# One transfer per weight tile from SyncE instead of two halves from SyncE and GpSimd, and the residual reloads moved to GpSimd's queue

## What is computed

```python
x = layernorm(x + attn(x))        # 16 heads, grouped (8 groups) qkv and output projections
x = layernorm(x + ffn(x))

def attn(x):   # q is scaled by 64 ** -0.5
    a = softmax(q @ k.T) @ v
    return grouped_linear(a, w_proj, b_proj)

def weight_quant(w):
    scale = 1.0 / clip(mean(abs(w)), 1e-05)
    return clip(round(w * scale), -1, 1) / scale

def act_quant(x):
    scale = 127.0 / clip(max(abs(x), -1), 1e-05)
    return clip(round(x * scale), -128, 127) / scale

def ffn(x):    # w_gate, w_up: 4096 x 1024, w_down: 1024 x 4096
    h = silu(act_quant(x) @ weight_quant(w_gate).T) * (act_quant(x) @ weight_quant(w_up).T)
    return act_quant(h) @ weight_quant(w_down).T
```

## Time and profile before

| | us |
|---|---|
| median of 2 runs | 2184.82 (2184.07 to 2185.58) |
| the profiled execution's own time | 2179.08 |
| its span on the slowest core (core 4) | 2177.4 |
| spans of the 8 cores | 2153.1 to 2177.4 |
| TensorE busy | 1348.4 (62%) |
| ScalarE busy | 948.9 (44%) |
| VectorE busy | 924.4 (42%) |
| GpSimd busy | 98.3 (5%) |

### The profile page before, as it was taken

One profiled execution on the slowest core, in us unless ns is written; L12 is line 12 of the kernel. 1 busy time (PEld: TensorE's weight loads), 2 busy tenths in 40 slices (PEclk: granted clock), 3 DMA queues, 4 the chain that ended last, 5 costly groups with the idle time before them and its releaser, 6 DMA issues.

```text
span 2177.4 us, 20832 instructions; the slowest of 8 cores (2153.1 to 2177.4 us)
## 1 busy us (share of the span) xinstructions
PE 1348.4 (62%) x5439; PEld 465.0 (21%) x5502; DVE 924.4 (42%) x1742; ACT 948.9 (44%) x1079; POOL 98.3 (5%) x180
## 2 busy tenths in 40 slices
PE   0057677567747670037673599964999737676682
PEld 0011111111111110011111244421444313222231
DVE  1148830635475323366345644444444441203023
ACT  1167788488838881018882022255112361001011
POOL 0000000001101111111110000000000000000000
PEclk9999888688858785558876799986999968888996
DMA  6789940136634666663651533334244416676672
GB/s 178 225 253 328 314 151 1 39 97 181 184 109 130 175 174 175 163 174 107 170 170 39 140 78 78 76 99 135 56 95 96 120 80 169 158 197 178 173 221 82
DMA packets 379140, 314.04 MB, mean 144 GB/s; under 512 B 298129, under 2 KB 300177, under 8 KB 376978
## 3 DMA queue, kind: packets, MB, share of 16 engines
q1 hardware_dynamic: 339712, 209.80, 37.2%
q0 software_dynamic: 16128, 54.54, 7.7%
q10 hardware_dynamic: 23186, 48.38, 6.5%
HBM read 161.49 MB, written 83.89 MB: 113 GB/s over the span
## 4 chain that ended last, share of the span: by engine, by line
PE 39%; DMA 18%; DVE 14%; ACT 13%; issue 7%; SPq 6%; ACTq 2%; DVEq 1%; POOL 0%; POOLq 0%
PE ps L84 39%; ACT A L84 12%; DVE A L84 10%; SPq L84 6%; DMA A<-wd 4%; DMA A<-wg 3%; DMA wdqT_s<-wtstage 2%; DVE ln_sb L84 2%; DMA wtstage<-wdq_s 2%; ACTq L84 2%; DMA wdt_sb<-wdqT_s 2%; DMA A<-wqkv 2%; DMA A<-wproj 1%; DMA xre_f<-xp_s 1%; DVE h L84 1%
## 5 line engine op out<-in xcount | busy, mean ns | idle before, releaser
L84 ACT ACTIVATE A<-ps,cst_sb 128x1024 bf16<-128x1024 f32 (+1 forms) x544 | 553.4, 1104 | 300.2 <-DVE A L84 209.8
L84 PE MATMUL ps<-A,A 64*128 64x512 bf16 (+1 forms) x2048 | 532.2, 434 | 205.6 <-ACT A L84 180.2
L84 PE MATMUL ps<-wg_sl,xqT 128*128 128x512 bf16 x1003 | 264.4, 408 | 114.6 <-DVE h L84 98.9
L84 PE MATMUL ps<-wdt_sb,hqT 128*128 128x512 bf16 x1003 | 243.6, 400 | 110.4 <-DMA wdt_sb<-wdqT_s 50.0
L84 PEld LDWEIGHTS ps<-A,A 64*128 64x128 bf16 (+1 forms) x2048 | 125.8, 106 | 610.1 <-issue 606.9
L84 ACT ACTIVATE A<-ps,scg 128x512 f32<-128x512 f32 x128 | 87.9, 687 | 331.5 <-PE ps L84 309.5
L84 DVE TENSOR_SCALAR A<-A,wsc 128x1024 f32<-128x1024 f32 x96 | 72.4, 754 | 280.1 <-DMA A<-wg 134.5
L84 DVE SCALAR_TENSOR_TENSOR h<-ps,scu,A 128x512 bf16<-128x512 f32 x128 | 96.1, 751 | 215.9 <-ACT A L84 211.7
L84 PE MATMUL ps<-wproj_sb,A 64*128 64x128 bf16 x256 | 36.4, 274 | 207.7 <-DVE A L84 207.7
L84 PEld LDWEIGHTS ps<-wg_sl,xqT 128*128 128x128 bf16 x1024 | 104.1, 103 | 251.8 <-issue 145.8
L84 DVE TENSOR_SCALAR A<-A 128x1024 f32<-128x1024 f32 (+1 forms) x208 | 144.4, 694 | 30.6 <-DVE A L84 20.0
(11 more groups left out here) (69 smaller groups left out, 756.0 us busy)
## 6 DMA issues: line engine op xcount, KB each, us to landing
wdt_sb<-wdqT_s SPq DMA_DIRECT2D x128, 256.0 KB, 3.5
A<-wg SPq DMA_DIRECT2D x32, 512.0 KB, 7.7
A<-wu SPq DMA_DIRECT2D x32, 512.0 KB, 7.0
A<-wd SPq DMA_DIRECT2D x32, 512.0 KB, 8.7
hq_s<-h ACTq DMA_DIRECT2D x16, 1024.0 KB, 3.9
A<-x SPq DMA_DIRECT2D x16, 512.0 KB, 7.2
xt_s<-A POOLq DMA_DIRECT2D x16, 512.0 KB, 3.8
A<-xt_s ACTq DMA_DIRECT2D x16, 512.0 KB, 3.6
```

The lines of the kernel that those rows point to most:

```text
L84: ins = getattr(eng, meth)(*args, **kw)
```

## The change

Three things, and nothing else for the kernel as it is run (`debug` is off):

1. The load of a weight-quantization unit is one DMA of 128x1024 floats (512 KB) from SyncE. GpSimd no longer issues a half or waits for `c_wq3`, and VectorE waits for one semaphore.
2. The loads of `xre_f` in `emit_down` and their waits go from ScalarE's list to GpSimd's.
3. The bias load has a semaphore of its own (`s_bp`), and waits for the constants ask for 16 instead of 32.

```diff
-    n = dma("scalar", A12[0:1, 0:1024], bproj_d[:, :], "s_cst")
+    n = dma("scalar", A12[0:1, 0:1024], bproj_d[:, :], "s_bp")
...
-    wait("tensor", "s_cst", 32)
+    wait("tensor", "s_bp", 16)
...
         if gidx >= 2:
             wait("sync", "c_wq3", 3 * (gidx - 1), future=True)
-            wait("gpsimd", "c_wq3", 3 * (gidx - 1), future=True)
         else:
             wait("sync", "c_wma", 96, future=True)
-            wait("gpsimd", "c_wma", 96, future=True)
-        dma("sync", stg[:, 0:512], tii[:, 0:512], f"s_wqp{par}")
-        dma("gpsimd", stg[:, 512:1024], tii[:, 512:1024], f"s_wqg{par}")
+        dma("sync", stg, tii, f"s_wqp{par}")
...
             wait("vector", f"s_wqp{par}", 16 * (gidx // 2 + 1))
-            wait("vector", f"s_wqg{par}", 16 * (gidx // 2 + 1))
...
-            wait("scalar", "s_xps0", 16 * (T // 2))
-            wait("scalar", "s_xps1", 16 * (T // 2))
+            wait("gpsimd", "s_xps0", 16 * (T // 2))
+            wait("gpsimd", "s_xps1", 16 * (T // 2))
             if gbase >= 1:
-                wait("scalar", "c_r2", gbase * 4, future=True)
-                wait("scalar", "c_s", c("c_s"))
-                wait("scalar", "s_out0", 16 * 2 * gbase)
-                wait("scalar", "s_out1", 16 * 2 * gbase)
+                wait("gpsimd", "c_r2", gbase * 4, future=True)
+                wait("gpsimd", "c_s", c("c_s"), future=True)
+                wait("gpsimd", "s_out0", 16 * 2 * gbase)
+                wait("gpsimd", "s_out1", 16 * 2 * gbase)
             for t4 in range(2):
-                E.dma("scalar", xre_f[:, t4 * 1024:(t4 + 1) * 1024],
+                E.dma("gpsimd", xre_f[:, t4 * 1024:(t4 + 1) * 1024],
                       xp_s[row0 + t4 * 128: row0 + (t4 + 1) * 128, :], "s_xre")
...
-                    wait("scalar", "c_r2", gbase * 4 + 2, future=True)
+                    wait("gpsimd", "c_r2", gbase * 4 + 2, future=True)
```

More of the change, by code:

```diff
@@ L501, in build @@
             wait("scalar", "m_qkv", c("m_qkv"))
-            wait("scalar", "s_cst", 32)
+            wait("scalar", "s_cst", 16)
             dap = dest[:, p * 2048 + qt * 512: p * 2048 + qt * 512 + 512]
@@ L708, in build @@
             if debug and qc >= 1:
-                wait("scalar", "s_dbg", c("s_dbg"))
+                wait("scalar", "s_dbgA", c("s_dbgA"))
             arp = A8[:, p * 512:(p + 1) * 512]
@@ L741, in build @@
         if debug:
-            wait("vector", "s_dbg", c("s_dbg"))
+            wait("vector", "s_dbgA", c("s_dbgA"))
         em("vector", "reciprocal", A10[:, 64:128], A10[:, 0:64], inc=("c_rcp", 1))
@@ L746, in build @@
             wait("sync", "c_pve", c("c_pve"))
-            dma("sync", dbg_ar[:, :], A8[:, :], "s_dbg")
+            dma("sync", dbg_ar[:, :], A8[:, :], "s_dbgA")
         if attn_lvl < 3 and attn_lvl not in (6, 7):
@@ L797, in build @@
                 wait("sync", "c_radd", c("c_radd"))
-                dma("sync", dbg_rc[:, :], A10[:, :], "s_dbg")
+                dma("sync", dbg_rc[:, :], A10[:, :], "s_dbgA")
             if attn_lvl != 4:
@@ L843, in build @@
         wait("sync", "s_dbg", c("s_dbg"))
-        wait("sync", "s_dbg", c("s_dbg"))
+        wait("sync", "s_dbgA", c("s_dbgA"))
     def wu_slice_ap(par, ic):
@@ L1050, in emit_down @@
                 if t4 == 2:
-                    wait("scalar", "c_r2", gbase * 4 + 2, future=True)
+                    wait("gpsimd", "c_r2", gbase * 4 + 2, future=True)
                     for t4b in range(2, 4):
-                        E.dma("scalar", xre_f[:, (t4b - 2) * 1024:(t4b - 1) * 1024],
+                        E.dma("gpsimd", xre_f[:, (t4b - 2) * 1024:(t4b - 1) * 1024],
                               xp_s[row0 + t4b * 128: row0 + (t4b + 1) * 128, :],
```

## The result

| | before | after |
|---|---|---|
| median, us | 2189.15 (8 runs) | 2127.13 (9 runs) |
| ratio, 95% interval | | 0.9714, 0.9681 to 0.9746 |
| span of the slowest core in the profiled execution | 2177.4 | 2120.8 |
| mean of the eight spans | 2164.6 | 2114.3 |

The change is 2.9% faster, some 62 us by the medians, where 26.5 us and 1.2% were forecast; 2127 lies under the range's lower end of 2130. The direction and the place were right, the size was not. Some executions are a few per cent longer, at a lower granted clock; the ratios and their intervals leave them out, the medians of this table don't, and e7's profile is of such an execution, so that only its cores 0 to 3, whose clock was not lower, are read.

A forecast was written before the change was run, and what follows sets the result against it. VectorE's weight units, waiting for transfers, were taken to hold up TensorE in blocks 1 and 2. Terms: 8.4 - 4.8 + 7.2 + 19.5 - 4.8 + 1.0 = 26.5 us, for a median of 2158 us, range 2130 to 2192.

The forecast's parts named there:

- The place and the edges: Weight units on VectorE hold up about 119 us of block 2 and 7.3 of block 1; block 3 isn't held up.
- Part 1, the unit load: Block 2, seven loads not behind transposes: one load landing in 4.8 us gains 1.2 us each, 8.4 us.
- Part 1, the load behind the transposes: Block 2, six loads behind the fourth transpose in SyncE's queue: twice the bytes, 0.8 us more each, -4.8 us.
- Part 2, the batches: Block 2, five later transpose batches: freed from the late store they fall from 17.4 to 13.5 us, 19.5 us gained.
- Block 1: Pairs of units sharing two buffers win 1.2 us each, 17 us, of which only 7.2 us can be had.
- Part 3: Down products, xre_f reloads moved to GpSimd: each of four groups waits 1.2 us longer, -4.8 us.
- +1.0: Start of the down products: the very first reload pair leaves its place where TensorE waits for down weights, 1 us gained.
- the wide load wins everywhere: Rival: loads behind transposes also land in 4.8 us (+14), batches give +23; 49 us gained, 2136 us; chance 0.18.

The follow-up runs named there:

- e7: Wide unit load alone, issued by GpSimd instead of SyncE, xre_f reloads left on ScalarE, against the kernel before: ratio 0.9966.
- e10: The kernel before with all 32 w_down transposes moved from block 2 to block 3: ratio 0.9714, block 2 at 243.8 us.
- e11: The changed kernel with all w_down transposes moved from block 2 to block 3: ratio to before 0.9531, block 2 at 222.0 us.
- e3: The kernel before with both 256 KB halves of the unit load issued by SyncE, none by GpSimd: ratio 0.9754, block 2 at 285.2 us.
- e9: The kernel before with the last store of a transpose batch moved ahead of GpSimd's next halves: ratio 0.9932, later batches 12.3 us.
- e4: e1 plus a GpSimd wait that keeps a batch's left-over store as late as before: ratio to before 0.9812, later batches 13.3 us.
- e2: The kernel before with only the xre_f reloads moved to GpSimd and the bias semaphore, keeping the two halves: ratio 0.9997.
- e5: The kernel before with four staging halves for the transposed w_down instead of two: ratio 0.9840, block 2 at 294.2 us.
- e1: The kernel before with only the wide unit load from SyncE, xre_f reloads left on ScalarE: ratio 0.9759, 2129.5 us.
- e12: The changed kernel with two transposes and five units (not four and six) per pair in block 2, three transposes in block 3: ratio to before 0.9460, 2065.7 us.
- e6: The changed kernel with four staging halves for the transposed w_down instead of two: ratio to before 0.9651, block 2 at 265.3 us.

## Why the prediction was wrong in size

- **The place and the edges** held. Blocks 1 and 2 were bound by the weight units, nothing of the gain in block 2 was hidden by attention, and block 3 didn't move. Three small readings were wrong and left the sum alone: block 3 has 24 units and not 22 (22 is the number of loads still to be issued), block 1 has 30, 15 pairs and not 14, and the later batches of core 4 go down to 15.65 us, not 17.21.
- **Part 1, the unit load.** The landing was taken at 4.8 us and measured at 4.7. A load that doesn't stand behind transposes was priced at 1.2 us; e10 and e11 give 1.0. In block 2 itself, what the batches and the loads behind them leave of the gain is 3.4 us, where 8.4 were forecast.
- **Part 1, the load behind the transposes, had the wrong sign.** The step said "it has twice the bytes now: 0.8 us more", -4.8 us in all. Taken from the timelines of all cores, the time from this load's issue on SyncE to VectorE's next unit is 7.1 us before (48 cases, 5.5 to 9.0), 5.4 after (4.6 to 6.2), and 5.4 in e3. It became 1.7 us shorter, a difference of 2.5 us six times: 15 us. The step went by one row, in which SyncE's half lands last, after 7.1 us. Over the 48 cases SyncE's half takes 5.9 us, GpSimd's lands last in 18, and VectorE waits for the later of the two. I had counted the bytes of the one transfer that I saw land last, and not those of GpSimd's halves for this unit and the next, which were open beside it. e3, where the same bytes come from SyncE alone in 5.4 us, shows that its being slow goes with the second issuer; whether because there is one more landing to wait for, or because the transfers slow each other, no run isolates.
- **Part 2, the batches, was undersized.** "I take 13.5 us, 0.8 above the first" was 11.6: 5 x 1.9 = 10 us more, and 1.1 less than the 12.73 that I had as the best bound. The step that failed is "each later batch should then look like the first". The first batch isn't a model for the others: without any halves from GpSimd it is still 12.8 us where the later ones are 11.6 (in the kernel before 13.4), and in e9, with the halves, 13.4 where they are 12.3. Its first transpose lands in 7.2 us in the changed kernel, those of the later batches in 5.9; why stays open. The halves just ahead of it, which I had overlooked, are worth only the 0.6 us from 13.4 to 12.8. That the store was late was only part of the mechanism: by e4 being late costs 1.9 us a batch. The other 4 us go with GpSimd's halves standing ahead of the stores, since e9 wins 5.2 of the 5.9 back with the halves still there, only later; how a half ahead of a store slows it is not shown.
- **Block 1** gave 5.0 us as a mean of the cores against 7.2, which was core 4's own and took for granted that the units would stop binding the block; on four cores they still do, by 2.0 to 4.2 us. The size isn't firm: the profiles with halves from both engines have block 1 at 221 to 230 us (before, e2, e5, e9, e10), those with SyncE alone at 216 to 217.
- **Part 3** was right for VectorE (3.6 us of waiting for 4.8) and wrong for the end, which didn't move. What balances it is that TensorE waits 2.6 us less for the down weights; e2 has this too, and e1 has not, so it comes from the moved reloads, for which the sum had +1.0.
- **The slowest core.** 6 us came from cores that differ less; the forecast had nothing for it. With these nearly all of the 56 us between the two profiled executions is accounted for; the 62 of the medians are 6 more because the profiled executions lie 10 and 4 us below their medians.

By the sum's own terms: 23 us were forecast for block 2 and 43 measured, 10 of the difference in the batches and 15 in the load behind them, less 5 elsewhere. The rival "the wide load wins everywhere" had the right sign for both and sizes that err in opposite ways (14 and 23 us against 10 and 29.5), and stood at 0.18. Against it I had set that the two transposes ahead of the load stay; they did, and the load was faster all the same.

The Trainium skill's rule ("DMA: Bandwidth & Descriptors", "Issuing engines are not separate DMA queues"), that issuing from several engines at once saves only the time of issuing, agrees with e3 in that the second issuer brings nothing: with both halves from SyncE the kernel is 2.5% faster than with two issuers. As a price it failed: by it the doubled load would land with GpSimd's half, in 5.6 us, and it took 4.7; the same 512 KB load issued by GpSimd in e7 took 5.3. And what a second issuer costs when its list and its queue are shared with stores that others wait for stands outside the rule and was most of the result.

## What to carry to other kernels

When one load is split over two issuing engines, price what else stands in the second engine's list and queue: here the halves delayed stores on which the first engine's next transposes waited, and that was worth more than the halves' own latency. A stretch of the trace is a model for the changed kernel only if nothing else sets it apart; my "first batch" was free of the late store, but it is 1.2 us longer than its followers in the changed kernel too. And a load's time is read from all its cases, not from the one in the chain: 7.1 us was one row, and the mean of that half 5.9. Where an engine waits long for a chain beside the main work, spreading that chain over the blocks that have room (e12) gives as much again as mending its links.

## What the runs showed that I had not expected

- A transposing DMA issued right behind another one holds SyncE longer, though no semaphore is waited for. After a wait for a store, as in the later batches before, the second transpose holds it for 1.2 us; right behind the first it takes 3.2 (first batch before), 2.7 (later batches after, and e6) and 3.7 (e5, with GpSimd's halves). No run tells what it waits for.
- Without GpSimd's loads the same bytes move in less time: 174 GB/s before and 227 after in the stretch of block 2 where TensorE stands still, and 185 against 229 in 690 to 820 us with no transposes of w_down (e10 on core 5, e11 on core 7).
